# Row maxima of an attention phase: two rows a unit by a product with a difference of keys, ScalarE's Relu and one VectorE pass, and semaphores cleared inside the next phase

## The reference, cut to what matters

```python
q = split_heads(embedding @ Wq + bq)      # 16 heads of width 8
k = split_heads(embedding @ Wk + bk)
v = split_heads(embedding @ Wv + bv)
scores = jnp.einsum('bhqd,bhkd->bhqk', q, k) * scale
attn = jax.nn.softmax(scores, axis=-1)
av = jnp.einsum('bhqk,bhkd->bhqd', attn, v)
```

## Time and profile before

| | |
|---|---|
| median of 3 runs | 1730.42 us (1728.12 to 1731.67) |
| the profiled execution, its own time | 1729.86 us |
| its span in the profile | 1728.1 us |
| PE busy | 1574.9 us, 91% |
| DVE busy | 1393.2 us, 81% |
| ACT busy | 1187.2 us, 69% |
| POOL busy | 787.9 us, 46% |
| mean granted TensorE clock | 0.961 of full |
| heads: first to last reduction of a row | 64.4 to 719.9 us |

### The profile page before, as it was taken

One profiled execution on the slowest core, in us unless ns is written; L12 is line 12 of the kernel. 1 busy time (PEld: TensorE's weight loads), 2 busy tenths in 40 slices (PEclk: granted clock), 3 DMA queues, 4 the chain that ended last, 5 costly groups with the idle time before them and its releaser, 6 DMA issues. The chain is left out here.

```text
span 1728.1 us, 41224 instructions
## 1 busy us (share of the span) xinstructions
PE 1574.9 (91%) x14986; PEld 806.7 (47%) x14986; DVE 1393.2 (81%) x2949; ACT 1187.2 (69%) x2461; POOL 787.9 (46%) x605
## 2 busy tenths in 40 slices
PE   6499999999999999968999998999999989699887
PEld 4122223223223232244777775667777755344454
DVE  6799999999999999646999996689999968343355
ACT  5168888888888888865788784267888744555421
POOL 4211111112221114247888882288888825644301
PEclk9589999999999999988999999999999999999999
DMA  5203111000000000111223222322232222000001
GB/s 166 75 20 129 34 36 38 20 20 20 21 20 20 21 22 17 49 51 39 59 57 83 61 54 62 80 53 62 57 92 62 55 57 66 1 1 2 1 18 32
DMA packets 124384, 79.14 MB, mean 46 GB/s; under 512 B 50594, under 2 KB 110940, under 8 KB 123932
## 3 DMA queue, kind: packets, MB, share of 16 engines
q1 hardware_dynamic: 122796, 75.44, 16.4%
q10 hardware_dynamic: 1392, 1.12, 0.2%
HBM read 42.82 MB, written 16.79 MB: 34 GB/s over the span
## 5 line engine op out<-in xcount | busy, mean ns | idle before, releaser
L1101 DVE TENSOR_REDUCE hd_top<-hd_pX 128x1 f32<-128x512 f32 x1024 | 623.6, 680 | 32.8 <-PE hd_pX L935 32.8
L1069 ACT ACTIVATE hd_E<-hd_pS 128x1024 f32<-128x1024 f32 x512 | 524.7, 1025 | 82.1 <-PE hd_pS L951 59.9
L935 PE MATMUL hd_pX<-l_K,l_Q 48*128 48x512 bf16 x1024 | 342.3, 396 | 26.1 <-DMA l_Q<-q_parts 21.5
L968 PE MATMUL hd_pO<-hd_E,l_V 128*32 128x256 f32 x4096 | 327.6, 392 | 18.0 <-ACT hd_O L1044 18.0
L951 PE MATMUL hd_pS<-l_Q,l_K 50*128 50x512 bf16 x1024 | 310.5, 384 | 3.0 <-DMA l_Q<-hd_negp 2.0
L883 POOL TENSOR_TENSOR hd_inv<-hd_OS,hd_minus 128x16 f32<-128x16 f32 x31 | 90.0, 2902 | 443.4 <-ACT hd_OS L1057 430.8
L1815 POOL TENSOR_TENSOR w_inv<-w_ss,w_mhalf 128x16 f32<-128x16 f32 x64 | 186.4, 2913 | 0.0
L1710 ACT ACTIVATE w_pS<-w_pS,w_nb 128x128 f32<-128x128 f32 x512 | 178.5, 365 | 6.5 <-DVE w_nb L1901 4.7
L1804 POOL TENSOR_TENSOR w_C<-w_C,w_N 128x1024 f32<-128x1024 f32 x64 | 151.0, 2360 | 61.3 <-DVE w_N L1875 61.0
L968 PEld LDWEIGHTS hd_pO<-hd_E,l_V 128*32 128x32 f32 x4096 | 81.7, 108 | 171.3 <-issue 124.7
L951 PEld LDWEIGHTS hd_pS<-l_Q,l_K 50*128 50x128 bf16 x1024 | 59.0, 94 | 197.8 <-issue 184.7
(11 more groups left out here) (290 smaller groups left out, 2785.0 us busy)
## 6 DMA issues: line engine op xcount, KB each, us to landing
w_VA<-w_V SPq DMA_DIRECT2D x127, 128.0 KB, 2.3
l_Q<-q_parts SPq DMA_DIRECT2D x192, 32.0 KB
l_K<-k_parts SPq DMA_DIRECT2D x168, 32.0 KB
m<-early_rows SPq DMA_DIRECT2D x64, 64.0 KB, 1.7
f_H<-m SPq DMA_DIRECT2D x32, 128.0 KB, 2.7
f_X<-m SPq DMA_DIRECT2D x16, 256.0 KB, 3.0
q_parts<-pj_ptq SPq DMA_DIRECT2D x8, 384.0 KB, 2.5
k_parts<-pj_ptk SPq DMA_DIRECT2D x8, 384.0 KB, 2.5
```

The lines of the kernel that those rows point to most:

```text
L935: nc.tensor.matmul(px[:, :], Q[m.j][rows, m.z, b, t * P:(t + 1) * P], K[m.j][rows, b, k * 512:(k + 1) * 512], start=True, stop=True).then_ ...
L968: last = nc.tensor.matmul(pO[VW * b:VW * b + VW, cols], V[n.j][:, b * NT + g, :], E[g % SLOTS][:, b, cols], start=(g == 0 and half == 0), ...
L1069: nc.scalar.activation(E[g % SLOTS][:, 2 * k:2 * k + 2, :], pS[k][:, :, :], ACT.Exp).then_inc(exped[k], 1)
L1101: nc.vector.tensor_reduce(top2[m.z][:, ROW_ORDER[q], k:k + 1], pX[slot][:, :], AX.X, ALU.max).then_inc(topped, 1)
```

## The change

Part 1: two rows of every unit (q = 3 and 7; in unit 0 q = 5 and 7, all of sequence 0) get their maximum in another way. With keys A (first 512) and B (second 512), max(qA, qB) = max(q(A - B), 0) + qB. The first cross of such a row multiplies with the difference of the keys, ScalarE writes its Relu to SBUF (`lead`), the second cross multiplies with B as before, and VectorE makes one pass that adds bank and `lead` and takes the maximum. The Relu stands in ScalarE's order right behind the exponential of the same step. The difference is made once by GpSimd in the projection, for sequence 0, split into three bfloat16 parts, stored, and loaded per head by six more DMAs behind those of Q and K. The bookkeeping of the ring (`Banks`) now keeps what each bank holds. The sums `OS` are copied without their unused columns (144 instead of 512).

Part 2: the sets of semaphores of the heads, the local layers and the linearised attention are cleared by GpSimd in the middle of the next phase, with no barrier; one pair of semaphores becomes one semaphore each, with counts that say the same.

```diff
+    def release(self):
+        self.signals.pop_all()
+        self.nc.clear_and_free_semaphores(self.handles)
...
@@ phase_l0_project, sync @@
+                sp.wait_ge(d_step, 4)
+                for part in range(3):
+                    sp.dma_start(d_parts[part], DP[part]).then_inc(d_stored, 16)
                 for j in range(2):
                     store(TURNS - 1, j)
+                sp.wait_ge(d_stored, 16 * 3)
@@ phase_l0_project, scalar @@
                             act.wait_ge(stored[n][j], 16 * i)
+                            if n == "k":
+                                act.wait_ge(differed, i)
                             nc.scalar.activation(F[n][:, j, :], pM[n][j][:, :], ACT.Identity, bias=b[:, :], scale=scale)
@@ phase_l0_project, gpsimd @@
+                    if j + 1 == len(K):
+                        for half in range(2):
+                            pool.wait_ge(taken["k"][half], 1)
+                        nc.gpsimd.tensor_tensor(DF, F["k"][:, 0, :], F["k"][:, 1, :], ALU.subtract).then_inc(differed, T // CH // 2)
...
+                pool.wait_ge(differed, T // CH // 2)
+                su = Step(pool, d_step, 4, 0)
+                su.then_wait(nc.gpsimd.tensor_copy(DP[0], DF))
+                su.then_wait(nc.gpsimd.tensor_tensor(DR, DF, DP[0], ALU.subtract))
+                su.then_wait(nc.gpsimd.tensor_copy(DP[1], DR))
+                su.done(nc.gpsimd.tensor_tensor(DP[2], DR, DP[1], ALU.subtract))
...
@@ phase_l0_heads @@
+        def lifted_rows(m):
+            return (5, 7) if m.n == 0 else (3, 7)
...
+            def load_d(eng, h, j, sem):
+                for band, parts in enumerate(PART_PAIRS):
+                    eng.dma_start(KD[j % 2][band * HD:band * HD + HD, :], d_parts[parts[1], bass.ds(h * HD, HD), :]).then_inc(sem, 16)
...
                     load(sp, h, j, K, k_parts, 1)
+                    load_d(sp, h, j, loaded[j])
...
-                for h in range(2):
-                    load(sp, h, h, Q, q_parts, 0)
+                load(sp, 0, 0, Q, q_parts, 0)
+                load_d(sp, 0, 0, first_d)
+                load(sp, 1, 1, Q, q_parts, 0)
+                load_d(sp, 1, 1, loaded[1])
@@ phase_l0_heads, tensor @@
-                    px = bank("top", TOPS * m.n + 2 * q + k)
-                    nc.tensor.matmul(px[:, :], Q[m.j][rows, m.z, b, t * P:(t + 1) * P],
-                                     K[m.j][rows, b, k * 512:(k + 1) * 512], start=True, stop=True).then_inc(crossed, 1)
+                    px = bank("lift" if lift else "top")
+                    keys = KD[m.j % 2][rows, :] if lift else K[m.j][rows, b, k * 512:(k + 1) * 512]
+                    nc.tensor.matmul(px[:, :], Q[m.j][rows, m.z, b, t * P:(t + 1) * P], keys, start=True, stop=True).then_inc(crossed, 1)
@@ phase_l0_heads, scalar @@
+                def lift_row(m, q):
+                    if q not in lifted_rows(m):
+                        banks.take()
+                        banks.take()
+                        return
+                    slot, _ = banks.take("lift")
+                    act.wait_ge(crossed, TOPS * m.n + 2 * q + 1)
+                    if banks.lifts > 2:
+                        act.wait_ge(topped, banks.paired[-3])
+                    nc.scalar.activation(lead[:, banks.lifts % 2, :], pX[slot][:, :], ACT.Relu).then_inc(lifted, 1)
+                    banks.take()
...
                             nc.scalar.activation(E[g % SLOTS][:, 2 * k:2 * k + 2, :], pS[k][:, :, :], ACT.Exp).then_inc(exped[k], 1)
                             if g == 1 and k == 0 and not n.is_first():
                                 take_sums(before)
-                        if in_stream(g, after, after2)[0].exists():
-                            pass_tops(TOPS // NT)
+                            m, row = in_stream(g, after, after2)
+                            if m.exists():
+                                lift_row(m, row + k)
@@ phase_l0_heads, vector @@
+                    if q in lifted_rows(m):
+                        banks.take("lift")
+                        slot, _ = banks.take()
+                        dve.wait_ge(crossed, TOPS * m.n + 2 * q + 2)
+                        dve.wait_ge(lifted, banks.lifts)
+                        nc.vector.tensor_tensor_reduce(pairs, pX[slot][:, :], lead[:, banks.lifts % 2, :], 1.0, LEAST, ALU.add, ALU.max,
+                                                       top2[m.z][:, ROW_ORDER[q], 1:2]).then_inc(topped, 1)
+                        return
...
@@ phase_layers, gpsimd @@
             feed.halves(pool)
+            ended.release()
@@ phase_ffn, gpsimd @@
+                    if n == 2:
+                        ended.release()
@@ build @@
-            heads.signals.close()
-            layers.signals.close()
-            mixer.signals.close()
```

More of the change, by code:

```diff
@@ L773, in exists, with take @@
                 return self.n < UNITS
+        def lifted_rows(m):
+            return (5, 7) if m.n == 0 else (3, 7)
         class Banks:
             def __init__(self):
[L780 to L785, removed]
+                self.at, self.held = 0, [None] * RING
+                self.tops, self.lifts, self.paired = 0, 0, []
+            def take(self, kind="top", m=None):
+                slot, held = self.at % RING, self.held[self.at % RING]
                 self.at += 1
-                self.last.append(kind)
-                return slot, held, back
+                if kind == "top":
+                    self.tops += 1
+                if kind == "lift":
+                    self.lifts += 1
+                    self.paired.append(self.tops + 1)
+                self.held[slot] = (kind, self.tops if kind == "top" else self.lifts if kind == "lift" else m)
+                return slot, held
         def units(emit):
@@ L913, in _, with bank @@
                 banks = Banks()
[L914 to L924, removed]
+                def bank(kind, m=None):
+                    slot, held = banks.take(kind, m)
+                    if held is None:
+                        return pX[slot]
+                    what, last = held
+                    if what == "top":
+                        pe.wait_ge(topped, last)
+                    elif what == "lift":
+                        pe.wait_ge(lifted, last)
+                    elif what == "neg":
+                        pe.wait_ge(neg_split[last.z], last.h + 1)
+                    else:
+                        pe.wait_ge(o_taken, last.n + 1)
                     return pX[slot]
@@ L971, in products, with close @@
                         last.then_inc(summed[g % SLOTS], 1)
-                def close(n, tops):
+                def close(n):
                     pe.wait_ge(o_ready, n.n + 1)
-                    px = bank("out", tops)
+                    px = bank("out", n)
                     for t in range(QT):
@@ L1026, in _ @@
                     products(last, NT - 1, half)
-                close(last, TOPS * UNITS)
+                close(last)
                 for k in range(2):
@@ L1113, in _ @@
                         fold(m)
-                        banks.take("neg")
+                        banks.take("neg", m)
                 def unit(n, before, after, after2):
@@ L1124, in unit @@
                         if g == TURN_AT and after.exists():
-                            banks.take("neg")
+                            banks.take("neg", after)
                         if g == CLOSE_AT and not n.is_first():
-                            banks.take("out")
+                            banks.take("out", before)
                 units(unit)
@@ L2370, in scalar, with phase_l1_attention @@
             self.norm(act, n - 7)
-def phase_l1_attention(nc, s, kept, start, following):
+def phase_l1_attention(nc, s, kept, start, following, ended):
     NT = S // P
@@ L2776, in build @@
             into_mixer = MixerStart(nc, mixer, kept)
-            phase_layers(nc, room, layers, kept, start, landed, feed, pad, into_mixer)
-            heads.signals.close()
-            layers.signals.close()
+            phase_layers(nc, room, layers, kept, start, landed, feed, pad, into_mixer, heads)
         early.close()
```

99 lines of the change are left out of this document (59 added, 40 removed).

## The result

The changed kernel takes 1784.6 us (median of 4 runs, 1781.3 to 1786.6) against 1731.1 for the kernel before (4 runs): a ratio of 1.031, 95% interval 1.029 to 1.033. The profiled execution took 1785.3 us with a span of 1783.5. Forecast were 1783 us and a range of 1747 to 1802.

The account below looks back on a forecast made before the run. DVE was taken to set the pace, with the other engines close behind. 1729.9 + 57 + 0.9 - 1.8 - 3.7 gave 1782 us, 1783 against the runs; range 1747 to 1802, at 75%.

Parts of the forecast that it names:

- DVE must stand for a full microsecond and gets back 0.60: Changed rows in the heads: cross to Relu's end takes 2.25 us or more against a lead of 1.21; one pass saves 0.60.
- The lead is 1.21: Ring of three banks: a cross can go out at most two reductions, 1.21 us, before its own turn on DVE.
- The lower end of the range: Milder slowdown in the heads: PE and ACT regain what they lose between the two rows, 23 us lost, 1747 us.
- Rival (a): Heads: the stand is swallowed and only DVE's sum of work counts, so 20 to 37 us faster there, 1688 to 1705; 11%.
- The failed step: Projection: GpSimd's subtraction of the keys has 5.9 us of room and the memsets it shifts end early, so it costs nothing.
- First pass: Three changed rows with no exponential beside them: cross to Relu's end is 1.02 us, so each gains 0.6, -1.8 in all.
- Units: Heads: about 1.9 us lost per unit, 57 us for thirty units with both rows, 0.9 for one with only q = 7.
- The clears' 3.7: Semaphore clears near 1480 and 1646 us: their stops of all engines go, 2.6 + 1.15 = 3.7 us gained, bounds 3 to 4.
- The loads of the difference: Six more DMAs per head on SP, 2.4 us, end 0.1 us before the next store of maxima, so nothing was taken.
- rival (d): Heads: the six added DMAs push the stores of maxima back, 30 us more, 1812 us; 6%.
- (e): Changed rows: VectorE makes the maximum in two instructions of full length, so nothing is saved, 1819 us; 3%.
- (f): Heads: the Relu reloads ACT's table, two loads of 1.28 us per Relu, 157 us in all; 2%.

## Why the prediction was right, and where it wasn't

**The mechanism and its size were right.** "DVE must stand for a full microsecond and gets back 0.60" is what the trace has, and more: the hand-worked timeline comes to stands of 2.08 (418.85 to 420.93) and 1.55 us (425.2 to 426.75), 2.04 and 1.45 are there; a unit of 22.2, there 22.12. Moving the Relu gives 49 us back, doubling it costs more, dropping one row leaves 0.51 a unit. It shows what carried the sum: following single crosses by offsets taken from the trace. The shares of busy time would have given a gain, for VectorE had less to do and ScalarE had room.

**"The lead is 1.21" was not right.** It is the most that three banks allow. At row q = 3 the lead is 0.25 us in both kernels, at q = 7 of the changed one 0.83 (cross at 412.81, VectorE free at 413.64): cross to pass, 2.29 and 2.28, less the lead is the stand. The sum didn't suffer, since it followed the crosses by the times of the rows. The lower end of the range did: it rests on a stand of 1.18 us in each row, which needs a lead of 1.21, and neither row had it.

**Rival (a), rates decide,** is out in this order of work. Its ceiling of 20 to 37 us in the units is about right all the same: the halved reductions gave 31 there. What it lacked is that the relief has to leave the crosses' timing alone. The Trainium skill, "Perfetto Trace Analysis", section "Optimizing Scalar/DVE Operations", allows offloading to Scalar when VectorE is saturated. Here it paid nothing with two rows a unit and the Relu in its better place (1.0021), and at most a few us with four. **The rule weighed** (the Trainium skill, "ScalarE: Activation LUTs", section "Rules for kernel authors", relu to VectorE, for its rate in bfloat16): these rows are float32, and the Relu took 592 ns on ScalarE, a reduction of as many columns 680 on VectorE. No run has a Relu on VectorE. What decided was the place, with 49 of the 53.5 us.

**The failed step:** "The later buffers' memsets shift by as much and end long before the phase does. ... Nothing." The room was worked out for the waits, and the contention was forgotten. Memsets pushed under a cast on VectorE made it 4.08 us, and the splitting on GpSimd slows four more instructions: +5.4 us in all in the profiled execution (3.9 to 5.4 in six), of which the later subtraction gave back a third to a half. The before trace had a hint that I didn't read: a cast of 1.47 us at 12.75 beside the memsets, where others take 0.43.

**Terms mis-sized.** First pass: -1.8 was said, with the Relu "inside the lead". The passes stood 0.33, 0.30 and 0.24 us, and from first reduction to first fold 0.35 us was gained of the 1.2 due. Units: 57.9 was said; 30 x 1.78 + 0.5 for the unit with only q = 7 (the run with one row) is 53.9. So 4.0 too much in the units, 1.5 too little in the first pass, 5.4 too little in the projection: 2.9 in all, and the span grew by 55.4 where 52.4 was said. That the sum came within 3 us is luck to this extent: with the units right it would have been 7 too low, still inside the range. The clears' 3.7 are there.

**Said of the profile after:** right were the pass (692 ns x64), its stand ended by the Relu, VectorE under 90% (83.6), and no barrier at the two places. The loads of the difference were hidden as said: in SP's timeline they end at 405.11, the store of maxima starts at 405.87, so rival (d) is out.

```profile
402.54 2.57 SPq L844 DMA_DIRECT2D l_D<-d_parts  x6
405.87 2.76 SPq L871 DMA_DIRECT2D l_Q<-hd_negp  x4
```

(e) and (f) are out by the counts: one pass a row, and one table load in the heads. Wrong was "ACT idle less than before in those steps": its wait for scores rose from 59.9 to 93.0 us over the phase, and between the two Relus it waited 0.66 and 0.48 us where the kernel before has five exponentials without a wait. TensorE's order was late as a whole.

**Open:** why the passes in the better order leave a unit at 20.50 us when the halved reductions allow 19.33. The short lead of the crosses, ScalarE's 0.59 us (worth 6.6 us of the run, with the scores' wait for exponentials) and waits that come up behind the passes all have a share. The runs don't part them further. An edit that issues the cross of the difference a half-step earlier wasn't tried.

## What to carry to other kernels

In a ring of few buffers, work that is moved to an engine with room costs by its place in that engine's order. Follow one item from producer to consumer, and compare the added latency with the lead that the trace shows at that very step, not with the ring's largest. Before any such move, cut the crowded engine's work by brute force once, as the halved reductions did: here it showed that even 38% off VectorE's reductions was worth 1.0 us a unit, because TensorE's order was next. And work given to GpSimd isn't free for VectorE: look for VectorE's casts in the stretch where GpSimd's memsets will land.

## What was unexpected in the hardware

- A VectorE cast of 128x512 (0.43 us) took up to 4.08 us beside GpSimd memsets (0.54 to 1.47 in the kernel before); operations of 0.69 us with two inputs kept their time beside memsets, but beside GpSimd's tensor operations they took 0.79 to 1.75, the longest with bfloat16 output.
- The result of VectorE's fused pass is read out by an instruction of its own of 0.08 us, which costs next to nothing: the next reduction starts 0.62 us after the pass's start, 0.60 after that of a reduction. The read of ScalarE's accumulator is 0.231.
- In the run with doubled Relus TensorE's stands were followed in 15 units by a stretch at the lower clock level, and the run lost some 20 us more than the stands themselves. The other units had the same stand and kept the full clock.
